# Keys and values of three of four images prepared inside the linear attention's program of a decoder kernel

## The reference, cut to what matters

```python
x = _layernorm(x + linear_attention(x, W_qkv, b_qkv, W_proj, b_proj, gamma, beta))
x = _layernorm(x + cross_attention(x, ctx_768, Wq, bq, Wk, bk, Wv, bv, Wo, bo))
x = _layernorm(x + gated_ffn_with_windowed_attention(x, ...))
```

```python
q = x @ Wq + bq                       # 512 queries an image
k = y @ Wk + bk                       # y: the context, 1601 x 192 an image
v = y @ Wv + bv
weight = softmax(q @ k.T / sqrt(32))  # 8 heads of 32 channels
out = (weight @ v) @ Wo + bo
```

## Time and profile before

| | |
|---|---|
| median of 3 runs | 2883.38 us (2878.19 to 2891.4) |
| the profiled execution, its time | 2882.24 us |
| its span in the trace | 2880.9 us |
| mean granted clock of PE | 0.881 |
| PE busy | 2227.3 us (77%) |
| DVE busy | 1720.4 us (60%) |
| ACT busy | 1181.4 us (41%) |
| POOL busy | 598.3 us (21%) |
| moved by DMA | 113.28 MB, mean 39 GB/s |

### The profile page before, as it was taken

The page is one execution under the profiler, slowest core; times in us unless marked ns, Lnnn a source line. Parts: engine busy times, 40 slices in busy tenths (PEclk is TensorE's granted clock), DMA queues, the critical chain, the costliest instruction groups (busy, mean ns, idle before and its releaser), DMA issues. The chain is left out here.

```text
span 2880.9 us, 41338 instructions
## 1 busy us (share of the span) xinstructions
PE 2227.3 (77%) x15516; PEld 1433.2 (50%) x15582; DVE 1720.4 (60%) x3425; ACT 1181.4 (41%) x2185; POOL 598.3 (21%) x488
## 2 busy tenths in 40 slices
PE   6995469897506999365589999996787787778777
PEld 3553137674404888334235555554455544455534
DVE  5676975467783333357456666661677652677663
ACT  2121664334331333121223555554566442566443
POOL 2220000001173455501310000000322142322052
PEclk9997579999657999687779999997899898899999
DMA  3001400100161111212431111102000001000000
GB/s 108 1 1 31 136 1 1 44 1 1 45 228 45 45 46 45 70 29 44 132 106 36 35 33 27 35 13 88 1 1 1 11 1 58 1 1 1 17 31 23
DMA packets 75010, 113.28 MB, mean 39 GB/s; under 512 B 22853, under 2 KB 59681, under 8 KB 74145
## 3 DMA queue, kind: packets, MB, share of 16 engines
q1 hardware_dynamic: 71744, 102.24, 11.8%
q0 software_dynamic: 3072, 8.39, 0.9%
HBM read 85.38 MB, written 31.20 MB: 40 GB/s over the span
## 5 line engine op out<-in xcount | busy, mean ns | idle before, releaser
L2338 DVE TENSOR_REDUCE xa_max<-psum 128x1 f32<-128x1024 f32 (+1 forms) x256 | 248.5, 988 | 130.0 <-PE psum L2211 129.3
L2444 ACT ACTIVATE xa_work<-psum 128x1024 f32<-128x1024 f32 (+1 forms) x208 | 212.7, 1023 | 188.6 <-PE psum L2234 186.7
L2249 PE MATMUL psum<-xa_work,xa_values 128*33 128x128 f32 (+1 forms) x3328 | 224.0, 277 | 0.0
L2249 PEld LDWEIGHTS psum<-xa_work,xa_values 128*33 128x33 f32 (+1 forms) x3328 | 168.1, 111 | 73.7 <-issue 70.2
L2644 PE MATMUL psum<-wqkv_l,x_hl_l 128*128 128x512 bf16 x538 | 136.9, 400 | 65.7 <-POOL x_hl_l L2904 32.9
L3010 PE MATMUL psum<-h_ch_f,w_f 128*128 128x512 bf16 (+1 forms) x556 | 134.9, 396 | 34.3 <-issue 13.1
L1623 DVE TENSOR_SCALAR moe_raw<-psum,tile_b 128x256 f32<-128x256 f32 x184 | 78.3, 475 | 138.9 <-PE psum L1465 137.9
L1719 POOL TENSOR_TENSOR x_ch<-moe_raw,x_ch 128x512 bf16<-128x512 f32 x92 | 105.4, 1156 | 151.9 <-ACT x_ch L1679 149.9
L1465 PE MATMUL psum<-moe_rows,moe_w 128*128 128x256 bf16 x1104 | 132.5, 278 | 3.0 <-POOL moe_rows L1715 3.0
L2234 PE MATMUL psum<-xa_query_rows,xa_key_rows 98*128 98x512 bf16 (+1 forms) x416 | 127.2, 388 | 8.4 <-ACT xa_work L2444 7.7
L2211 PE MATMUL psum<-xa_key_rows,xa_query_rows 96*128 96x512 bf16 (+1 forms) x512 | 127.0, 344 | 4.5 <-DVE xa_max L2338 2.4
(11 more groups left out here) (415 smaller groups left out, 4934.7 us busy)
## 6 DMA issues: line engine op xcount, KB each, us to landing
xa_key_rows<-cross_keys SPq DMA_DIRECT2D x48, 200.1 KB, 3.5
moe_raw<-in_moe_w SPq DMA_DIRECT2D x16, 512.0 KB, 4.8
x_ch<-in_moe_w SPq DMA_DIRECT2D x16, 512.0 KB, 4.7
cross_keys<-xa_work SPq DMA_DIRECT2D x4, 1601.0 KB, 5.7
moe_rows<-slots_in SPq DMA_DIRECT2D x23, 256.0 KB, 2.8
slots_out<-moe_rows SPq DMA_DIRECT2D x23, 256.0 KB, 2.1
ctx_f<-in_ctxT SPq DMA_DIRECT2D x2, 2401.5 KB, 15.3
xa_work<-in_ctxT SPq DMA_DIRECT2D x4, 800.5 KB
```

The costliest lines, as they stand in the source:

```text
L2249: ins = pe.matmul(total.ap[a * LANE:a * LANE + VC, c:c + PIECE], t["v"][b][0:rows, kt, first + a, :], exps[0:rows, a, c:c + PIECE], start= ...
L2338: v.tensor_reduce(t["maxes"][n % 2][:, qt * HU + a, part:part + 1], u.wide[:, 0:c1 - c0], AX.X, ALU.max).then_inc(*u.free)
L2444: act.activation(t["exps"][k % EXPS][0:rows], u.wide[0:rows].rearrange("p (m q) -> p m q", q=T), ACT.Exp, scale=1.0 / float(np.sqrt(np.flo ...
```

## The change

The keys and values of images 0, 1 and 2 (`AHEAD = B - 1` images) are computed inside the linear attention's program. A side list of 46 steps (weights, and for each image the casts `parts`, the splits `context`, four `keys`, two `rows` and seven `value`) is dealt out evenly between the 26 steps behind the first two of `linear_plan`, so that every engine's queue has them in between. They use banks of their own, the two double banks 0 and 2. Their context, halves and keys have tiles in the linear program, one buffer of each context half and a keys' tile for each half of the channels; values of three images and the split weights are in tiles that live through both programs. To make room, `la_out` goes (the projected rows of image b are written over its part of `x_ch`, which PE has read by then) and `la_rg` shrinks from four to two images. The keys are stored to HBM from the linear program, each half of the channels by itself.

The cross program loads only Wq, image 3's context and Wo. Splitting of x gets a step of its own (`x_split`), with two buffers for the split x and the queries. Images 0 and 1 ask first, with image 3's context between; the queries of images 2 and 3 and image 3's keys and values (21 steps) are mixed with the first 27 maxima. POOL's fills stand behind `x_split` of image 1.

The diff, cut to its core:

```diff
@@ linear_plan
+    side = [("weights",)] + flat([[("parts", b), ("context", b)] + key_steps(b) + value_steps(b) for b in range(AHEAD)])
+    return plan[:2] + mingle(plan[2:], side)
+AHEAD = B - 1
+def key_steps(b):
+    return flat([[("keys", b, o, c0) for c0 in range(0, S2, 2 * BANK)] + [("rows", b, o)] for o in range(HALVES)])
+def value_steps(b):
+    return [("value", b, kt) for kt in range(0, KT, 2)]
@@ linear_attention
-                 o_tok=..., o_ch=..., a_tok=sb("la_out", [P, TILES, D]),
-                 rg=ring("la_rg", B, [P, HALVES, T]))
+                 o_tok=..., o_ch=..., rg=ring("la_rg", 2, [P, HALVES, T]), **kept)
+        t.update(w_f=sb("xa_w_f", [P, 4, D]), ctx_f=sb("xa_ctx_f", [P, 2, S2]), c_high=..., c_low=..., c_both=...,
+                 k_hl=[sb("xa_k_hl%d" % n, [P, 2, S2], BF16)[:] for n in range(2)])
+        use.update(m.banks([p for p in plan if p[0] in ("keys", "value")], (0, 2)))
@@ linear_sp
+    for n, name in enumerate(("k", "v")):
+        sp.dma_start(t["w_f"][:, 2 * n, :], dram["xa_" + name][0:P, :]).then_inc(*s.xw_loaded.up(16))
+        for r in (0, CTX_B):
+            sp.dma_start(t["w_f"][r:r + CTX_B, 2 * n + 1, :], dram["xa_" + name][P:DC, :]).then_inc(*s.xw_loaded.up(16))
+    context_sp(m, s, t, 0)
+    for step in plan:
+        if kind == "regroup":
...
+            sp.wait_ge(*s.rg_stored.now())
+            if b > 1:
+                sp.wait_ge(*use["project", b - 2, TPB - 1].full)
...
+        elif kind == "context" and b + 1 < AHEAD:
+            sp.wait_ge(*s.a_low(b + 1))
+            sp.wait_ge(*s.b_low(b + 1))
+            context_sp(m, s, t, b + 1)
+        elif kind == "rows":
+            rows_sp(m, s, t, use, step)
+def rows_sp(m, s, t, use, step):
+    b, o = step[1:]
+    for c0 in (0, 2 * BANK):
+        sp.wait_ge(*use["keys", b, o, c0].done)
+    sp.dma_start(dram["cross_keys"][b].rearrange("x (o p) s -> o p x s", p=P)[o], t["k_hl"][o]).then_inc(*keys_stored(s, o).up(16))
@@ linear_dve, step "project" (and the same place of x_ch in "close")
-            a = t["a_tok"][:, b * TPB:(b + 1) * TPB, :]
+            tiles = [projected(m, b)[:, n // 2, n % 2, :] for n in range(TPB)]
@@ linear_pool
+    for n in range(AHEAD):
+        g.memset(t["v"][n][:, :, :, NX:VC], 1.0).then_inc(*s.v_ones.up())
+        if kind == "context":
+            g.wait_ge(*s.closed.now())
+            context_pool(m, s, t, b)
@@ prepare_pe, new, used by both programs (keys; value is alike)
+        if (o, c0) == (0, 0):
+            pe.wait_ge(*s.a_low(b - first + 1))
+            pe.wait_ge(*s.b_low(b - first + 1))
+        pe.wait_ge(*u.empty)
...
@@ prepare_act, new
+    elif kind == "parts":
+        act.wait_ge(*s.ctx_loaded(16 * 3 * (n + 1)))
+        if n:
+            act.wait_ge(*use["value", b - 1, KT - 1].full)
+        act.copy(t["c_high"][:, 0:S2], t["ctx_f"][:, 0, :]).then_inc(*s.c_split.up())
+        act.copy(t["c_both"][:, 0:S2], t["ctx_f"][:, 1, :]).then_inc(*s.c_split.up())
+    elif kind == "keys":
+        if b > first and c0 == 0:
+            act.wait_ge(*keys_stored(s, o)(16 * (b - first)))
...
@@ cross_plan
+    def asked(b):
+        return [("x_split", b)] + [("queries", b, c) for c in range(HALVES)] + [("asked", b)]
-    plan = [("context", 0)] + prepare(0) + prepare(1) + prepare(2) + mingle(prepare(3), maxima[:lead])
+    rest = asked(2) + asked(3) + flat([key_steps(b) + value_steps(b) for b in range(AHEAD, B)])
+    plan = asked(0) + [("parts", B - 1), ("context", B - 1)] + asked(1) + mingle(rest, maxima[:lead])
@@ cross_sp
+    sp.dma_start(t["w_f"][:], dram["xa_q"].rearrange("(h p) o -> p h o", h=2)).then_inc(*s.w_loaded.up(16))
+    context_sp(m, s, t, B - 1)
+        if kind == "asked":
...
+            if b == 0:
+                sp.wait_ge(*s.q_stored0(16))
                 for u in range(3):
                     load(u)
@@ cross_pool
+        elif kind == "x_split":
...
+            g.tensor_tensor(t["x_hl"][b % 2][:, 1], m.x_ch[:, :, b * T:(b + 1) * T], t["x_hl"][b % 2][:, 0], ALU.subtract).then_inc(*s.x_low.up())
+            if b == 1:
+                g.wait_ge(*s.x_low.now())
                 for n in range(3):
                     g.memset(t["k_rows"][n][SPLIT:ROWS_X], 1.0).then_inc(*s.ones.up())
...
@@ build
+        with ExitStack() as both:
+            kept = dict(v=[...], wk=..., wv=...)
+            linear_attention(m, kept)
+            cross_attention(m, kept)
```

More of the change, by code:

```diff
@@ L1759, in linear_attention @@
         steps = []
-        for kind, b in plan:
+        for step in plan:
+            kind, b = step[0], step[-1]
             if kind == "inputs":
@@ L1773, in linear_attention, with linear_sp @@
         linear_act(m, s, t, use, plan, nth)
-        linear_pool(m, s, t, plan)
-        settle(m, [use["channels", B - 1, h].done for h in range(HALVES)])
-def linear_sp(m, s, t, use):
+        linear_pool(m, s, t, plan, use)
+        settle(m, [use["channels", B - 1, h].done for h in range(HALVES)] + [use["value", AHEAD - 1, KT - 1].done]
+               + [s.k_stored0.now(), s.k_stored1.now(), s.v_ones.now()])
+def linear_sp(m, s, t, use, plan):
     sp, dram = m.nc.sync, m.dram
@@ L1931, in linear_act @@
     act.wait_ge(*s.ones(2))
-    for kind, b in plan:
-        if kind == "inputs":
+    for step in plan:
+        kind, b = step[0], step[-1]
+        if kind in PREPARED:
+            prepare_act(m, s, t, use, step, 0)
+        elif kind == "inputs":
             if b > 1:
@@ new lines, in prepare_act @@
+def prepare_act(m, s, t, use, step, first):
+    act, kind = m.nc.scalar, step[0]
+    if kind == "weights":
+        act.wait_ge(*s.xw_loaded(16 * 6))
+        for src, high, low, rows in weight_parts(t):
+            act.copy(high, src).then_inc(*s.w_high.up())
+    elif kind == "parts":
+        b, n = step[1], step[1] - first
+        act.wait_ge(*s.ctx_loaded(16 * 3 * (n + 1)))
[3 more added lines that the diff above has]
+        act.copy(t["c_both"][:, 0:S2], t["ctx_f"][:, 1, :]).then_inc(*s.c_split.up())
+    elif kind == "keys":
+        b, o, c0 = step[1:]
+        u, c1 = use[step], min(c0 + 2 * BANK, S2)
+        if b > first and c0 == 0:
+            act.wait_ge(*keys_stored(s, o)(16 * (b - first)))
+        act.wait_ge(*u.full)
+        act.activation(t["k_hl"][o][:, 0, c0:c1], u.wide[:, 0:c1 - c0], ACT.Identity, bias=m.col("xa_bk", o)).then_inc(*s.in_high.up())
@@ L1992, in cross_plan @@
 def cross_plan():
-    def prepare(b):
-        return ([("queries", b, c) for c in range(HALVES)]
-                + [("keys", b, o, c0) for o in range(HALVES) for c0 in range(0, S2, 2 * BANK)] + [("rows", b)]
-                + [("context", b + 1)] * (b + 1 < B) + [("value", b, kt) for kt in range(0, KT, 2)])
+    def asked(b):
+        return [("x_split", b)] + [("queries", b, c) for c in range(HALVES)] + [("asked", b)]
     maxima = []
@@ L2128, in cross_sp @@
         kind = step[0]
-        if kind == "context" and step[1] + 1 < B:
-            context(step[1] + 1)
-        elif kind == "rows":
+        if kind == "asked":
             b, = step[1:]
```

356 lines of the change are left out of this document (183 added, 173 removed).

## The result

The kernel after takes 2875.96 us, the median of 7 runs (2873.35 to 2879.23), beside 2889.62 us for 7 runs of the kernel before on the same chip: ratio 0.996, interval 0.9941 to 0.9978. It is faster, by 0.4% instead of the forecast's 0.76%. The profiled execution took 2878.78 us around a span of 2877.5, only 3.4 us under that of before.

The account below looks back on a forecast made before the run. It took DVE's queue, with PE and ACT in it, to bound the linear stretch, no engine being full. Linear stretch +42 and head -63.9 gave -21.9 us, so 2861 us, range 2840 to 2882.

Parts of the forecast that it names:

- That this stands for is left as it is: Steady stretch, PE 96 of 100 us busy at full clock: unchanged, so any gain must be won before it.
- in the steady stretch nothing should differ: Sign to check in the profile: the stretch behind the first softmax score stays the same, a change of nothing.
- The linear stretch, 42: Linear attention: three images' keys and values lengthen it by 42 us through DVE's queue, bounds 20 to 72.
- the walk's 6, 13.5, 22, 24, 33.5 and 37 us: Step-by-step lateness of DVE in the linear attention, from the start of inputs 2 to the last copies to channels.
- 14 us of new waits: Linear stretch: DVE waiting three times 3.8 us after context splits, less cover, and some 5 us for wide banks.
- 3 for POOL's block: Linear stretch: DVE's three context splits each stretched by 1 us while POOL works, 3 us in all.
- 14 less 9: Linear stretch: 14 us of new DVE waits less 9 us of old idle time that the new work fills.
- an equal price for each image: Linear stretch: each image moved in costs DVE the same work, 10.9 us, three 32.7 us.
- The head, -63.9: Cross attention's head: first softmax score 79.6 us after the linear program's last copy instead of 143.5; bounds 57 to 71.
- POOL's fills on the path: Head: POOL's 8.2 + 1.2 us of fills stand before x_split of image 2, whose queries wait until X + 30.
- rival 2: Linear stretch grows by 50 to 70 us through waits: about no change, 2868 to 2890; 0.21 together with another rival.
- Rival 3: Linear stretch: each image takes its whole 23.4 us, POOL blocks DVE for 12; slower, 2902 us; chance 0.06.

Follow-up runs that it names:

- e7: The kernel after with the square root for images 0 to 2 spread as 14 DVE instructions over 14 steps, scaling and turn 13 steps later: 2846.14 us, ratio 0.9888.
- e9: e7 with the keys and values of two images instead of three computed in the linear program: 2849.66 us, ratio 0.9883.
- e1: The kernel after run again, unchanged: 2881.28 us, ratio 0.9982.
- e2: The kernel after with POOL's fills of ones and zeros moved one step earlier, behind x_split of image 0: 2878.36 us, ratio 0.9971.
- e10: e7 with the lower part of the context's second half subtracted on DVE instead of POOL in the linear program: 2853.55 us, ratio 0.9898.
- e6: The kernel after with the steps that need the variance's root one step later at each image's end: 2861.91 us, ratio 0.9952.
- e4: The kernel after with the cross attention norm's square root on DVE, in one block of four Newton steps, instead of ACT: 2882.94 us, ratio 0.9991.

## Why the prediction was right in one part and wrong in two

**"That this stands for is left as it is", "in the steady stretch nothing should differ":** this step failed, and it is the largest miss. The instructions are the same, but their time is not: a hole of 2.56 us was there three times, costing little more than itself, and in the kernel after the clock is down for 13.6 us behind each, where it is down for only 3.4 us behind one of them in the kernel before. The profiled difference (-3.4) falls 18.5 us short of the forecast (-21.9): 14.7 here, 7.6 in the linear stretch, less 0.2 in the head and 3.6 outside of both programs. I had read the earlier trace rows, PE 96 of 100 us busy at clock 1.00, as a property of the stretch. That window even held one of the three holes, from 1669.3 to 1671.9, with no fall behind it: 3.6 us of idle PE at full clock said nothing of what the same hole would cost once the order ahead of it had moved. The Trainium skill (TensorE: Matmul & The Clock Gate, HAM oscillation) describes short matmul bursts between waits that throttle the array again and again. Its case has bursts shorter than the waits. These rows show the same for a wait of 2.56 us in a PE that is otherwise nearly full: 16.1 us of lost clock for 7.7 us of waits (e7 against after). The same page (What's actually happening) has the point at which the clock first rises vary from run to run; the falls here lay at the same 140, 260 and 380 us in three executions of after's order.

**The linear stretch, 42:** the mechanism (DVE's queue, stretched by work and by waits at each context) was right, its size was short by 7.6 us. The miss was not one event. Against the walk's 6, 13.5, 22, 24, 33.5 and 37 us, the milestones came late by 8.9 (inputs 2), 17.8 (end of inputs 3), 26.4, 30.0 and 40.8 (projects 1 to 3) and 46.7 (last copy). The term that was mis-sized is "14 us of new waits". DVE's busy time in the stretch, before and after, and its inserted steps that waited, with the idle time before them last:

```profile
1240.30:1387.20 146.90, 93.01 (x352) 61.49 (x352) 95.27 (x276) 35.33 (x72) 10.28 (x4) 0.83 0.16 29
```

```profile
1237.00:1433.50 196.50, 152.43 (x667) 83.21 (x667) 128.71 (x316) 56.15 (x94) 19.27 (x7) 0.88 0.29 73
```

```profile
L2123 DVE TENSOR_TENSOR xa_values<-psum,rows 128x512 f32<-128x512 f32 (+1 forms) x21 | 13.2, 647 | 7.5 <-PE psum L2098 7.4
L2117 DVE SCALAR_TENSOR_TENSOR xa_k_hl<-psum,cols,xa_k_hl 128x1024 bf16<-128x1024 f32 (+1 forms) x12 | 12.6, 1052 | 18.2 <-ACT xa_k_hl L2148 18.1
```

DVE is busy 33.4 us more, where 34 and 3 for POOL's block stood; the work was sized well. It is idle 16.2 us more (67.8 instead of 51.6), where 14 less 9 stood. The inserted steps alone waited 26.6 us, not 14: 18.2 before the keys, 7.5 before the values, 0.9 before a context. The filled idle time came out near, 10.4 instead of 9. Before the first keys of images 0 and 1 it was 6.05 and 6.11 us, where I took 3.8. The 3 us for POOL's block were near: one closing addition took 4.25 us instead of 1.22 and one of the three subtractions of a context 3.06 instead of 1.83, 4.3 us together. And an equal price for each image was wrong: e9 has 28.0 for the third and 18 to 22 for the first two together. That it is so because the input steps that hid those are over by then, and PE runs at 0.74, fits the order but has no run of its own. The clock over 0.9 that I expected did not come for the whole stretch (0.88, and 0.82 in e1); DVE's 130 us (128.7) did, and PE's 140 to 150 nearly (152.4). Between executions the growth itself moves: with before at 146.9 and 150.7, after at 196.5 and 199.5, it is 46 to 53 us.

**The head, -63.9:** right, -64.1, and by its steps but for the last wait of the first queries (DVE's half of Wq, not POOL). That it came out to 0.2 us is partly luck: one kernel has 79.4 and 74.5 in two executions, with PE's clock at 0.76 and 0.84 in it, so the gain is 64 to 69. Costing POOL's fills on the path was right as a description, and e2 shows that it was not a price: without them the next queue, ACT's, held the same step.

**The rivals.** The measured time, 2875.96, lies outside the forecast's 2848 to 2872 and inside rival 2's 2868 to 2890, but not for rival 2's reason alone: its growth of 50 to 70 was only touched at its edge, and the larger part of the miss came from elsewhere. Rival 3's block of 12 us by POOL didn't occur. None of the four had the time lost in a stretch without an edit.

**The sum.** The three stretches together are 782.7 and 786.7 us in two executions of before, and 782.9, 781.0 and 781.0 in three of after's order (e2's fills among them): some 3 us. The timed runs have 11.6 us by the ratio (6 to 17 by its interval; the medians are 13.7 apart), and e1's 5 (0 to 11). Where the rest lies no run shows: ahead of the linear attention, in code that both share, two executions of the kernel before alone are 12.8 us apart (1240.3 and 1227.5).

## What to carry to other kernels

A stretch that a change doesn't edit can still pay for it: look there for holes in a nearly full PE, ask what each costs if the clock falls behind it, and take them out before judging a change that shifts them. A clock of 1.00 in a window that holds such a hole is no proof that it stays up when the order moves. When work is moved under other work, price each piece by what is left to hide it at its place: here the first two images were cheap and the third was worth nothing. And before removing a wait, read who is next in line; twice here (e2, e10) the wait was real and its removal gave 1 us or none.

## What the runs showed of the hardware that I had not expected

A hole of 2.56 us in PE's work, with PE busy 18.7 of the 20 us that end 1.0 us into it, is followed by 13.6 us at 1.2 GHz in one order of the same work, by about half that in another (e6, one execution), and by none or 3.4 us in a third (before). The first and the third did so again in the next executions. What in the order decides stays open: e6 shows that the hole's place matters, not by which rule, and e4 that a longer hole need not bring a longer fall. The root in one block of 14 dependent DVE instructions of 4 columns made a hole of 4.60 us in PE's work, where the two table loads of 1.28 us and the root between them had made 2.56; with one instruction in each step no such hole is left. And a DVE instruction on 128x4 elements that takes 0.16 us alone took 1.98 beside POOL's addition, up to that one's end: the size of an instruction doesn't protect it from the block.
